# Three slots of modulated rows, and the second half's splits and stacks moved into attention, in the first block of an adaLN transformer kernel

## The chip, the cores and the metric

The kernel runs on one core of one Trainium2 chip. The metric is the device time of one execution in microseconds, as a median over runs. The engines are TensorE (PE, with its weight loads PEld), VectorE (DVE), ScalarE (ACT), GpSimd (POOL) and SyncE (SP), which here only issues transfers and waits. Each engine works through its own program in order; they meet at semaphores. Transfers are issued on the queue of the engine that issues them (SP or GpSimd) and run on 16 DMA engines.

## The reference

A transformer layer with adaptive layer norm over x of 8 blocks x 512 rows x 256 columns: relative-bias attention with 16 heads of 16, then a mixture of 8 experts of which each token takes 2. Six modulation vectors of 256 come for each block from one small product:

```python
mod = (_silu(L0_c) @ L0_wmod).reshape(L0_c.shape[0], 6, 1, -1)
sa, ca, ga, sb, cb, gb = (mod[:, 0], mod[:, 1], mod[:, 2], mod[:, 3], mod[:, 4], mod[:, 5])
ga = (2 * (ga >= 0) - 1) * jnp.maximum(jnp.abs(ga), 0.25)   # gb likewise
h = _layernorm(x, axis=-1) * (1 + ca) + sa
x = x + ga * attention(h)          # softmax(q k / 4 + bias[rel]) v, then W_out
h = _layernorm(x, axis=-1) * (1 + cb) + sb
x = x + gb * experts(h)            # top 2 of 8, gelu, layer norm, residual
```

## The kernel before

The kernel is four blocks of engine programs, one after the other: `prepare`, `attention`, `route`, `experts`. No engine starts a block before all have ended the one before. The change touches `prepare` and the first batch of `attention`.

`prepare` normalises and modulates the 8 blocks of x. For block b VectorE takes the moments of four 128-row tiles (`moments(b)`, L344 and L347), GpSimd raises variance to the power -0.5 (`deviations(b)`, L260 and L262), VectorE makes the offsets (`offsets(b)`, L352), ScalarE normalises the tiles (`normal(b)`, L297), TensorE transposes them (`turn(b)`, L456), and VectorE and ScalarE each apply scale and shift to one half of the transposed rows (`modulate(b)`, L359 and L305). Block 0 goes to a buffer that stays (`ahead.h1`); blocks 1 to 7 go to one of two slots of `ht`, from where GpSimd's queue stores them to `h1t` (`store_h(b)`, L268). A slot is used again when its store has landed (`stores_of_slot`).

Beside this, block 0's projections are made for the first batch of attention: TensorE multiplies q and k in halves (`project(k)`, L473; names `q0 k0 q1 k1 v0 v1` for k = 0 to 5), ScalarE adds the bias (`project_out`, L138), VectorE splits each result into three bf16 parts (`split(k)`, four passes, L368 to L374), SP stores the parts to `splits` (`store_parts`, L121) and, when the parts of one q and one k half have landed, loads them back as stacks of 96 rows (`load_stack`, L130: 6 loads for `qs`, 6 for `ks`, 128 KB each). Heads 0 to 7 use half 0, heads 8 to 15 half 1. SP also loads the bias rows of the heads as `s_tile`, four heads to a group (`load`, L151); groups 0 and 1 are loaded in `prepare`, 2 and 3 at the start of `attention`.

The modulation vectors are made twice. The columns for scale and shift come from sixteen small matmuls into `ps_col` (L489). The rows, which attention reads back from DRAM as `mod_rows`, come from three products of 512 columns (`mod(j)`, L481) into the one bank `ps_mod`, after `turn(3)`, `turn(4)` and `turn(5)` (`MOD_AFTER`); ScalarE copies each to `rows` (`copy_rows`, L317) after `modulate(2)`, (3) and (4), and VectorE makes the gates from them at the end (L433 to L443). SP then stores all six (L240) and waits until they have landed (`rows_stored`); that is SP's end of the block. GpSimd's end is the landing of all h1t stores. GpSimd also moves v into place and reloads h1 of block 1 (L272, L288), after `store_h(3)`.

In `attention` a batch is one block with 16 heads, n = 0 to 15. For each head TensorE makes four score tiles (L1183), VectorE adds the bias and takes the row minimum (L997), GpSimd and ScalarE subtract it, two tiles each (`lower`, L835 and L926), TensorE transposes (`turn_scores`, L1197, for head n - 1 in the time of head n), ScalarE takes exp (L934), TensorE weighs (L1211). GpSimd has further work at fixed places beside the heads (`beside(b, n, kind)`): it makes the splits of q and k for the next batch (`split_high`, `split_low`, L747 to L757) at n = 2 to 3.5 and 9.5 to 11, and at n = 5 it begins to split a piece of the expert weights (`piece_high(b, 0)`, L766, which waits for `w_piece_in[0]`). SP loads these pieces (`load_pieces`, L659). The order in SP's program for the first batch:

```python
if kind == "first":
    sp.wait_ge(h1_in, 16)
    for group in range(2, GROUPS):
        ahead.load(sp, ext_rows, group)
load_pieces(b, 0)
```

In GpSimd's program the work beside a head comes ahead of that head's subtractions: `beside(b, n, kind)`, `lower(b, n, 0)`, `lower(b, n, 1)`, `beside(b, n + 0.5, kind)`.

Of the kernel before, what the change touches and what calls it, by code (L numbers as in the profile page):

```python
# [158 lines left out]
def prepare(nc, ahead, x, c_t, wmod, rel_rev, w_qkv, b_qkv, w_out, b_out, gate_t, expert_bias, mod_rows, ext_rows, splits, h1t):  # L159

    with ExitStack() as ctx:  # L161
# [22 lines left out]
        ht = sb("ht", [P, 2, DC, S])  # L184
# [16 lines left out]
        h_out = [sem("h_out0"), sem("h_out1")]  # L201
        MOD_AFTER = (3, 4, 5)
        block = ctx.enter_context(nc.Block())

        def h1_of(b):

            return ahead.h1 if b == 0 else ht[:, b % 2, :, :]

        def stores_of_slot(b):

            return (b - 1) // 2 * 16 if b > 0 else 0

        @block.sync
        def _(sp):
# [8 lines left out]
            for b in range(1, B):  # L223
                load_x(b)

# [4 lines left out]
            ahead.load_weights(sp, w_qkv, b_qkv, w_out, b_out, gate_t, expert_bias)  # L230
# [13 lines left out]
        def _(pool):  # L244
# [19 lines left out]
            def store_h(b):  # L264

                pool.wait_ge(h_dve, b + 1)
                pool.wait_ge(h_act, b + 1)
                pool.dma_start(h1t[b, :, :, :], ht[:, b % 2, :, :]).then_inc(h_out[b % 2], 16)  # L268
# [8 lines left out]
            for b in range(1, B):  # L277
# [3 lines left out]
                if b == 3:  # L281
# [5 lines left out]
                    pool.wait_ge(h_out[1], 16)  # L287
                    pool.dma_start(ahead.h1[:, :, :], h1t[1, :, :, :]).then_inc(ahead.h1_in, 16)  # L288
            pool.wait_ge(h_out[0], 16 * (B // 2 - 1))
            pool.wait_ge(h_out[1], 16 * (B // 2))  # L290

        @block.scalar
        def _(act):
# [6 lines left out]
            def modulate(b):  # L300
# [3 lines left out]
                at_least(act, h_out[b % 2], stores_of_slot(b))  # L304
# [9 lines left out]
            def copy_rows(j):  # L314

                act.wait_ge(mod_ready, j + 1)
                act.activation(rows[:, j * 512:(j + 1) * 512], ps_mod[0:B, :], ACT.Copy).then_inc(rows_copied, 1)  # L317
# [3 lines left out]
            normal(0)  # L321
            normal(1)
            modulate(0)
# [15 lines left out]
        def _(dve):  # L339
# [15 lines left out]
            def modulate(b):  # L355

                dve.wait_ge(t_done, b + 1)
                at_least(dve, h_out[b % 2], stores_of_slot(b))
# [24 lines left out]

            dve.wait_ge(exp_done, 1)
# [17 lines left out]
            offsets(1)  # L402
            dve.wait_ge(cols_ready, 2)
            modulate(0)
            moments(2)
# [15 lines left out]
            split(2)  # L421
# [9 lines left out]
            dve.wait_ge(rows_copied, 3)  # L431
            for k, g in enumerate((2, 5)):
# [1597 lines left out]
```

## Time and profile before

| | us |
|---|---|
| median of 3 runs | 1262.36 |
| lowest, highest | 1259.53, 1264.88 |
| the profiled execution | 1260.16 |
| its span, first to last instruction | 1258.4 |
| first instruction of attention, from the span's start | 72.70 |
| TensorE's mean granted clock, as a share of 2.4 GHz | 0.942 |

The profile is of one execution; times inside it count from the span's start, and 1.8 us lie around the span. TensorE is busy for 1105.8 us (88%), VectorE for 790.0, GpSimd for 752.1, ScalarE for 632.7. A busy share over the whole span mixes the four blocks, so the stretches are read one by one. In the rows below an engine's idle time stands in brackets with what ended it; "DMA share" is the mean busy share of the 16 DMA engines, which can pass 1 when transfers overlap.

### The profile page before, as it was taken

The numbers are of one execution on the slowest core, as the hardware profiler recorded it, in microseconds if no ns is written. First come the engines' busy times: TensorE is split into PE (matmuls) and PEld (weight loads), VectorE is DVE, ScalarE is ACT, GpSimd is POOL, SyncE is SP. The second block draws the span as 40 slices with busy tenths as digits, with TensorE's granted clock in tenths as the row PEclk, the third lists the DMA queues.
The fourth block names the chain that finished last, engine by engine and source line by source line (L and its number), as shares of the span: only waits on it lengthen the run. The fifth ranks groups of instructions, "written<-read, shape, count | busy, mean of one in ns | idle before, by whom it ended". The sixth has DMA issues, their size and how long they took to land. (4 is left out here: it accounts for less than half of the span.)

```text
span 1258.4 us, 30706 instructions
## 1 busy us (share of the span) xinstructions
PE 1105.8 (88%) x11290; PEld 881.2 (70%) x11291; DVE 790.0 (63%) x2150; ACT 632.7 (50%) x905; POOL 752.1 (60%) x845
## 2 busy tenths in 40 slices
PE   5569999999999999999999826999999999999920
PEld 3237777777777777777777613888888888888820
DVE  4636668667676685776867676555555555555577
ACT  3538776776777777767677500222222222222222
POOL 2347497687776886759757521454554445554556
PEclk9779999999999999999999955999999999999965
DMA  8976754863557537555473156243434244242364
GB/s 281 297 217 181 209 154 109 198 143 100 142 144 173 146 92 187 144 112 171 90 185 102 68 170 183 42 113 49 117 44 111 46 117 115 44 112 46 50 172 138
DMA packets 124364, 167.18 MB, mean 133 GB/s; under 512 B 14520, under 2 KB 100792, under 8 KB 124256
## 3 DMA queue, kind: packets, MB, share of 16 engines
q1 hardware_dynamic: 107168, 137.59, 40.2%
q0 software_dynamic: 17088, 28.14, 12.1%
q8 instruction: 68, 1.11, 0.4%
q14 instruction: 40, 0.33, 0.1%
HBM read 105.26 MB, written 60.44 MB: 132 GB/s over the span
## 5 line engine op out<-in xcount | busy, mean ns | idle before, releaser
L997 DVE CUSTOM_DVE_ANT_0 b_sn<-b_ps_s,s_tile 128x512 f32<-128x512 f32 x512 | 341.3, 688 | 185.1 <-PE b_ps_s L1183 181.9
L934 ACT ACTIVATE b_pt<-b_ps_t 128x1024 f32<-128x1024 f32 x256 | 259.4, 1017 | 74.0 <-PE b_ps_t L1197 74.0
L1197 PE MATMUL b_ps_t<-ident,b_sn 128*128 128x128 f32 x2048 | 268.2, 273 | 3.1 <-POOL b_sn L835 1.3
L1197 PEld LDWEIGHTS b_ps_t<-ident,b_sn 128*128 128x128 f32 x2048 | 237.2, 141 | 41.0 <-issue 10.8
L1804 ACT ACTIVATE d_g<-d_ps_u 128x512 f32<-128x512 f32 x156 | 92.7, 598 | 308.2 <-PE d_ps_u L1930 300.2
L835 POOL TENSOR_SCALAR b_sn<-b_sn,b_mn 128x512 f32<-128x512 f32 x256 | 175.1, 695 | 97.2 <-DVE b_mn L997 96.7
L1759 POOL DMA_INDIRECT sums<-d_yo,d_places x78 | 132.4, 1698 | 166.2 <-ACT d_yo L1813 147.8
L926 ACT ACTIVATE b_sn<-b_sn,b_mn 128x512 f32<-128x512 f32 x256 | 181.9, 722 | 90.0 <-DVE b_mn L997 83.4
L1930 PE MATMUL d_ps_u<-d_xp,k_wu 128*128 128x256 bf16 x1776 | 202.0, 274 | 0.0
L1183 PE MATMUL b_ps_s<-s_ks,s_qs 96*128 96x512 bf16 x512 | 179.0, 386 | 24.8 <-PEq L161 14.7
L1945 PE MATMUL d_ps_y<-k_wd,d_gp 128*128 128x256 bf16 x1776 | 199.9, 273 | 0.0
L1930 PEld LDWEIGHTS d_ps_u<-d_xp,k_wu 128*128 128x128 bf16 x1776 | 173.5, 98 | 22.2 <-issue 0.4
L1945 PEld LDWEIGHTS d_ps_y<-k_wd,d_gp 128*128 128x128 bf16 x1776 | 173.8, 98 | 20.0
L1211 PE MATMUL b_ps_o<-b_pt,s_v 128*32 128x128 f32 x4096 | 138.4, 276 | 0.1
L1211 PEld LDWEIGHTS b_ps_o<-b_pt,s_v 128*32 128x32 f32 x4096 | 104.0, 109 | 40.8 <-ACT b_pt L934 36.8
L1842 DVE CAST d_xp<-d_ps_x 128x512 bf16<-128x512 f32 x39 | 26.9, 691 | 150.7 <-PE d_ps_x L1917 150.7
L1866 DVE TENSOR_TENSOR d_gp<-d_g,d_gp 128x512 bf16<-128x512 f32 x156 | 108.0, 692 | 5.4
L1739 POOL DMA_INDIRECT k_xg<-h_rows,d_tokens x76 | 76.0, 1000 | 43.5 <-POOL d_tokens L1735 31.8
L1864 DVE CAST d_gp<-d_g 128x512 bf16<-128x512 f32 x156 | 66.6, 427 | 39.3 <-ACT d_g L1804 35.9
L1183 PEld LDWEIGHTS b_ps_s<-s_ks,s_qs 96*128 96x128 bf16 x512 | 43.8, 98 | 57.2 <-DVE b_mn L997 36.2
L772 POOL TENSOR_TENSOR b_w_split<-b_w_raw,b_w_split 128x1024 bf16<-128x1024 f32 x32 | 68.8, 2148 | 0.0
L1228 PE MATMUL b_ps_m<-s_h,s_wqkv 128*128 128x512 f32 x112 | 54.4, 609 | 0.0
(239 smaller groups left out, 1126.2 us busy)
## 6 DMA issues: line engine op xcount, KB each, us to landing
w_parts<-b_w_split SPq DMA_DIRECT2D x32, 512.0 KB, 3.8
splits<-s_parts SPq DMA_DIRECT2D x32, 384.0 KB, 3.3
s_qs<-splits SPq DMA_DIRECT2D x96, 128.0 KB, 5.8
s_ks<-splits SPq DMA_DIRECT2D x96, 128.0 KB, 7.3
b_w_raw<-in_w_up_t SPq DMA_DIRECT2D x16, 512.0 KB, 10.8
b_w_raw<-in_w_down_t SPq DMA_DIRECT2D x16, 512.0 KB, 7.1
k_wu<-w_parts SPq DMA_DIRECT2D x8, 1024.0 KB, 4.9
k_wd<-w_parts SPq DMA_DIRECT2D x8, 1024.0 KB, 7.4
```

The source lines that it names most:

```text
L835: pool.tensor_scalar(sn[:, n % 2, t, :], sn[:, n % 2, t, :], -1.0, mn[:, n % 2, t:t + 1], ALU.mult, ALU.add).then_inc(lower_pool, 1)
L926: act.activation(sn[:, n % 2, t, :], sn[:, n % 2, t, :], ACT.Identity, bias=mn[:, n % 2, t:t + 1], scale=-1.0).then_inc(lower_act, 1)
L934: act.activation(pt[:, m, 2 * pair:2 * pair + 2, :], ps_t[:, 2 * pair:2 * pair + 2, :], ACT.Exp).then_inc(exped, 1)
L997: dve.tensor_tensor_reduce(sn[:, n % 2, t, :], ps_s[:, t % 2, :], ahead.tile[:, n, at:at + S], -1.0, BIG, ALU.add, ALU.min, mn[:, n % 2, t ...
L1183: pe.matmul(ps_s[:, t % 2, :], qs[:, half, m, t * P:(t + 1) * P], ks[:, half, m, :], start=True, stop=True).then_inc(scored, 1)
L1197: mm = pe.transpose(ps_t[:, j, t * P:(t + 1) * P], sn[:, m, t, j * P:(j + 1) * P], ident[:, :])
L1211: mm = pe.matmul(ps_o[2 * DK * t:2 * DK * (t + 1), n % TB * P:(n % TB + 1) * P], v[:, j, n, :], pt[:, n % 2, j, t * P:(t + 1) * P], start= ...
L1759: pool.indirect_dma_start(sums, bass.IndirectOffsetOnAxis(ap=places[:, u, i:i + 1], axis=0), yo[:, u, i, :], None, compute_op=ALU.add).the ...
L1804: act.activation(g[:, j, :], ps_u[:, j, :], ACT.Gelu).then_inc(gelued, 1)
L1866: dve.tensor_tensor(gp[:, u, 1, at], g[:, j, :], gp[:, u, 0, at], ALU.subtract).then_inc(g_split, 1)
L1930: mm = pe.matmul(ps_u[:, j // 2, j % 2 * ROWS:(j % 2 + 1) * ROWS], kept.wu[:, slot, w, c, j * P:(j + 1) * P], xp[:, u, x, c * ROWS:(c + 1) ...
L1945: mm = pe.matmul(ps_y[:, i, 0:D], gp[:, u, x, j * ROWS + i * P:j * ROWS + (i + 1) * P], kept.wd[:, slot, w, j, :], start=(j == 0 and n == ...
```

## The change

- `ht` gets three slots instead of two; block b uses slot (b - 1) % 3.
- SP issues `load_weights` (five small loads: biases, gate, w_out) between the loads of x for blocks 3 and 4, instead of after tile group 0.
- ScalarE does `modulate(0)` ahead of `normal(1)`, VectorE `modulate(0)` ahead of `offsets(1)`.
- TensorE multiplies a zeroed slot of `ht`, six times 128x512 before the column products and once after `turn(0)`; VectorE zeroes the slot first of all.
- The rows of modulation are two products instead of three (columns 512 to 1535), into `ps_mod` and `ps_col`, both after `turn(3)`; ScalarE copies them after `normal(5)`; the gates are made before `modulate(7)`; SP stores four of the six vectors, columns 512 on.
- GpSimd moves v and reloads h1 after `store_h(5)` instead of `store_h(3)`. Its `deviations` keep their places.
- The splits k = 2 and 3 of block 0 leave VectorE; GpSimd makes them in the first batch of attention at n = 0.5 and 1.5. SP stores them and loads the stack of half 1 at the start of that batch, ahead of tile groups 2 and 3 and of the first expert weights.

```diff
-        ht = sb("ht", [P, 2, DC, S])
+        HT = 3
+        ht = sb("ht", [P, HT, DC, S])
...
             for b in range(1, B):
                 load_x(b)
+                if b == 3:
+                    ahead.load_weights(sp, w_qkv, b_qkv, w_out, b_out, gate_t, expert_bias)
...
-            ahead.load_weights(sp, w_qkv, b_qkv, w_out, b_out, gate_t, expert_bias)
...
-            for k in range(2, 4):
-                ahead.store_parts(sp, splits, 0, k, k + 1)
-            ahead.load_stack(sp, splits, 0, 1)
             sp.wait_ge(rows_done, 1)
-            sp.dma_start(mod_rows, rows[:, :]).then_inc(rows_stored, 16)
+            sp.dma_start(mod_rows[:, 2 * D:], rows[:, 2 * D:]).then_inc(rows_stored, 16)
...
-                if b == 3:
+                if b == 5:
                     pool.wait_ge(ones_set, 1)
                     pool.wait_ge(v_out, 2)
...
             normal(0)
+            modulate(0)
             normal(1)
-            modulate(0)
...
             for b in range(3, B):
                 normal(b)
+
+                if b - 2 == MOD_AFTER:
+                    for j in range(2):
+                        copy_rows(j)
                 modulate(b - 1)
-                if b in MOD_AFTER:
-                    copy_rows(MOD_AFTER.index(b))
...
             moments(1)
-            offsets(1)
             dve.wait_ge(cols_ready, 2)
             modulate(0)
+            offsets(1)
...
             moments(6)
-            split(2)
             modulate(4)
             offsets(6)
             moments(7)
-            split(3)
             modulate(5)
             offsets(7)
             modulate(6)
+            make_rows()
             modulate(7)
...
+            def warm(n):
+
+                for _ in range(n):
+                    pe.matmul(ps_mod[:, :], ht[:, 2, 0, 0:P], idle, start=True, stop=True)
+
+            pe.wait_ge(idle_set, 1)
+            warm(WARM_FIRST)
             pe.wait_ge(silu_done, 1)
...
             turn(0)
+            warm(WARM_NEXT)
...
             for b in range(3, B):
                 turn(b)
-                if b in MOD_AFTER:
-                    mod(MOD_AFTER.index(b))
+                if b == MOD_AFTER:
+                    for j in range(2):
+                        mod(j)
...
                 if kind == "first":
 
+                    for k in range(2, 4):
+                        ahead.store_parts(sp, splits, 0, k, k + 1)
+                    ahead.load_stack(sp, splits, 0, 1)
                     sp.wait_ge(h1_in, 16)
                     for group in range(2, GROUPS):
                         ahead.load(sp, ext_rows, group)
...
                 first, last = kind == "first", kind == "last"
+                if first and n in (0.5, 1.5):
+                    split_high(2 + int(n), 2 + int(n), 0)
+                    split_low(2 + int(n), 2 + int(n))
```

## Rows read from the trace of the kernel before

**Rows 1.** Busy us by stretch and engine, granted clock, DMA share, GB/s.

```profile
60.00:65.00 5.00, 0.00 (x0) 0.00 (x0) 3.25 (x10) 0.50 (x1) 0.53 (x1) 0.50 1.14 168
...
100.00:150.00 50.00, 50.00 (x609) 37.94 (x608) 32.54 (x97) 39.28 (x49) 34.40 (x40) 1.00 0.71 218
```

**Rows 2.** Waits of SP and ScalarE to 85 us: total, times, longest.

```profile
SPq L127 <- DMA splits<-s_parts: 14.2, 2, 10.2
...
SPq L161 <- DMA mod_rows<-a_rows: 6.7, 1, 6.7
...
ACT a_rows L317 <- PE a_ps_mod L481: 10.2, 3, 4.0
```

**Rows 3.** Timeline of SP's queue: start, us of issuing, line, transfer, count.

```profile
27.15 3.96 SPq L121 DMA_DIRECT2D splits<-s_parts  x2
...
35.14 3.54 SPq L130 DMA_DIRECT2D s_qs<-splits  x6
...
41.67 2.15 SPq L151 DMA_DIRECT2D s_tile<-ext_rows  x4
...
58.44 3.15 SPq L130 DMA_DIRECT2D s_qs<-splits  x6
...
72.70 4.08 SPq L151 DMA_DIRECT2D s_tile<-ext_rows  x8
```

**Rows 4.** Stretches of 2 us, columns as in group 1.

```profile
44.00:46.00 2.00, 0.00 (x0) 0.00 (x0) 1.97 (x10) 2.00 (x5) 0.47 (x1) 1.00 1.12 158
...
52.00:54.00 2.00, 0.31 (x3) 0.32 (x4) 0.00 (x0) 2.00 (x5) 0.00 (x0) 1.00 1.02 416
...
152.00:154.00 2.00, 2.00 (x9) 0.99 (x8) 1.31 (x4) 1.28 (x3) 0.00 (x0) 1.00 1.18 131
```

**Rows 5.** Timeline of the first 30 us: start, us, engine, line, idle before.

```profile
14.87 0.36 DVE L347 BATCH_NORM_AGGREGATE a_mv<-a_stats 128x2 f32<-128x6 f32 x4
...
16.91 2.07 ACT L297 ACTIVATE a_xt<-a_xt,a_less,a_rstd 128x256 f32<-128x256 f32 x4 [4.86 <-DVE a_less L352]
...
19.79 5.49 PE L473 MATMUL a_ps_q<-s_h,s_wqkv 128*128 128x512 f32 x8 [5.21 <-ACT s_h L305]
...
24.36 0.43 DVE L368 CAST s_parts<-s_qf 128x512 bf16<-128x512 f32 x1 [5.16 <-ACT s_qf L138]
...
25.99 3.60 PE L473 MATMUL a_ps_q<-s_h,s_wqkv 128*128 128x512 f32 x8
```

**Rows 6.** Timeline, the last modulation of VectorE.

```profile
59.72 0.81 DVE L359 TENSOR_SCALAR a_ht<-a_ps_t,a_scale,a_shift 128x512 f32<-128x512 f32 x1 [3.63 <-DMA h1t<-a_ht]
```

**Rows 7.** DMA issues 40:50, 72:90: KB, us to landing; landings of h1t.

```profile
s_tile<-ext_rows SPq DMA_DIRECT2D x4, 448.0 KB, 11.9
...
splits<-s_parts SPq DMA_DIRECT2D x1, 384.0 KB, 2.5
...
DMA to landing us min/median/max: 3.7/4.2/8.5
```

**Rows 8.** Timeline of the first batch of attention, GpSimd and TensorE.

```profile
74.67 1.37 POOL L835 TENSOR_SCALAR b_sn<-b_sn,b_mn 128x512 f32<-128x512 f32 x2 [1.87 <-DVE b_mn L997]
...
96.38 1.06 POOL L766 CAST b_w_split<-b_w_raw 128x1024 bf16<-128x1024 f32 x1
...
98.92 1.37 POOL L835 TENSOR_SCALAR b_sn<-b_sn,b_mn 128x512 f32<-128x512 f32 x2 [1.49 <-DVE b_mn L997]
...
101.80 1.04 PE L1197 MATMUL b_ps_t<-ident,b_sn 128*128 128x128 f32 x8
...
116.67 0.61 POOL L747 CAST s_parts<-s_qf 128x512 bf16<-128x512 f32 x1 [0.36 <-ACT s_qf L138]
...
119.39 1.17 POOL L757 TENSOR_TENSOR s_parts<-s_rest,s_parts 128x512 bf16<-128x512 f32 x1
```

**Rows 9.** GB/s in 40 slices of 60:72, then of 72:90 us.

```profile
GB/s 263 379 191 106 157 133 116 137 161 106 137 157 106 126 222 184 205 358 427 386 393 365 314 167 140 171 150 171 147 164 157 150 188 133 174 147 65 55 0 0
...
GB/s 0 0 0 56 135 271 175 159 287 374 422 350 271 342 335 414 422 414 366 327 406 440 414 398 382 422 401 427 427 428 419 410 355 55 0 0 0 0 239 341
```

More of the change, by code:

```diff
@@ L200, in prepare @@
         bq_scaled, projected, qk_out, v_out = sem("bq_scaled"), sem("projected"), sem("qk_out"), sem("v_out")
-        h_out = [sem("h_out0"), sem("h_out1")]
-        MOD_AFTER = (3, 4, 5)
+        h_out = [sem("h_out0"), sem("h_out1"), sem("h_out2")]
+        MOD_AFTER = 3
+        WARM_FIRST, WARM_NEXT = 6, 1
+        idle = ht[:, 2, 0, :]
+        idle_set = sem("idle_set")
         block = ctx.enter_context(nc.Block())
         def h1_of(b):
-            return ahead.h1 if b == 0 else ht[:, b % 2, :, :]
+            return ahead.h1 if b == 0 else ht[:, (b - 1) % HT, :, :]
         def stores_of_slot(b):
-            return (b - 1) // 2 * 16 if b > 0 else 0
+            return (b - 1) // HT * 16 if b > 0 else 0
         @block.sync
@@ L285, in _ @@
                         move_v(half)
-                    pool.wait_ge(h_out[1], 16)
+                    pool.wait_ge(h_out[0], 16)
                     pool.dma_start(ahead.h1[:, :, :], h1t[1, :, :, :]).then_inc(ahead.h1_in, 16)
-            pool.wait_ge(h_out[0], 16 * (B // 2 - 1))
-            pool.wait_ge(h_out[1], 16 * (B // 2))
+            for slot in range(HT):
+                pool.wait_ge(h_out[slot], 16 * len(range(slot + 1, B, HT)))
         @block.scalar
@@ L316, in copy_rows @@
                 act.wait_ge(mod_ready, j + 1)
-                act.activation(rows[:, j * 512:(j + 1) * 512], ps_mod[0:B, :], ACT.Copy).then_inc(rows_copied, 1)
+                act.activation(rows[:, (j + 1) * 512:(j + 2) * 512], (ps_mod, ps_col)[j][0:B, :], ACT.Copy).then_inc(rows_copied, 1)
             act.wait_ge(c_in, 16)
@@ L382, in values, with make_rows @@
                                   ahead.b_v[:, :].unsqueeze(1).to_broadcast([P, 2, D]), ALU.add).then_inc(v_out, 1)
+            def make_rows():
+                dve.wait_ge(rows_copied, 2)
+                for k, g in enumerate((2, 5)):
+                    dve.tensor_scalar(sgn[:, k, :], rows[:, g * D:(g + 1) * D], 0.0, 2.0, ALU.is_ge, ALU.mult).then_inc(rows_step, 1)
+                for g in (4,):
+                    dve.tensor_scalar(rows[:, g * D:(g + 1) * D], rows[:, g * D:(g + 1) * D], 1.0, None, ALU.add).then_inc(rows_step, 1)
+                dve.wait_ge(rows_step, 3)
+                dve.tensor_scalar(sgn[:, :, :], sgn[:, :, :], -1.0, None, ALU.add).then_inc(rows_step, 1)
+                dve.wait_ge(rows_step, 4)
+                for k, g in enumerate((2, 5)):
+                    dve.tensor_tensor(rows[:, g * D:(g + 1) * D], rows[:, g * D:(g + 1) * D], sgn[:, k, :], ALU.mult).then_inc(rows_step, 1)
+                dve.wait_ge(rows_step, 6)
+                for k, g in enumerate((2, 5)):
+                    last = dve.scalar_tensor_tensor(out=rows[:, g * D:(g + 1) * D], in0=rows[:, g * D:(g + 1) * D], scalar=0.25,
+                                                    in1=sgn[:, k, :], op0=ALU.max, op1=ALU.mult)
+                last.then_inc(rows_done, 1)
+            dve.memset(idle, 0.0).then_inc(idle_set, 1)
             dve.wait_ge(exp_done, 1)
```

27 lines of the change are left out of this document (7 added, 20 removed).

## The prediction, written before the change was run

> **What bounds the kernel now.** I read the busy time by stretches first [rows 1]: from 100 us on TensorE is busy for 50.00 of 50 us, so whatever moves the start of attention moves the end by as much, and whatever stops TensorE there is lost in full. From 60 to 65 us TensorE does nothing and its granted clock is 0.50, the 1.2 GHz level: the first block waits for something else. The waits of the queue engine say for what [rows 2]: SP waits 10.2 us for two stores of split rows (half 1), then 6.7 us for mod_rows to land, and then the second block begins. SP's own timeline gives the order [rows 3]: stack of half 0 at 35.14, four bias tiles at 41.67, stack of half 1 only at 58.44, second block at 72.70. The bytes [rows 4] say why this is slow: while a stack of 12 loads is under way the core moves 158 GB/s (44 to 46 us) or 131 (152 to 154 us), with the DMA engines busy; otherwise 416.
>
> **The first block, part by part.**
> Early order. ScalarE no longer puts normal(1) ahead of modulate(0). Block 0's rows are complete when VectorE's modulate(0) ends; it now follows moments(1) at 15.2 us [rows 5], so at 16.0 instead of 19.7, and TensorE's q and k products, at 19.79 before [rows 5], start at about 16.1. ScalarE's normal(1) keeps 16.91 to 18.98, its first q output comes at 19.0 instead of 23.6, VectorE's split(0) at 19.75 instead of 24.36 [rows 5]: 4.6 us. Split(1) then ends near 26.2 instead of 30.7.
> Load_weights goes ahead of the loads of blocks 4 to 7: five issues of some 0.5 us and 0.56 MB, 1.4 us at 416 GB/s [rows 4]. Those four loads, the store of ext and tile group 0 move back by that much; block 4's moments come at 27 us, 7 us after its rows land, so I take nothing. The second store of split rows waits for split(1) and goes out at 27.1 instead of 31.1 [rows 3], but now behind group 0's 1.8 MB; it lands near 32 (35.1 before). So the stack of half 0 starts 3 us earlier.
> Idle products. Six of 128x512: at 0.86 us an instruction and two instructions each they end by 11.9 us at the latest, at most 2.6 us after w_mod (9.2). The columns are then done by 14.5, under the cover of moments(1), which hold VectorE to 15.2. Their use is that q and k run at 2.4 GHz: the eight instructions took 5.49 us at 19.79, after 5.2 us without work, and 3.60 at 25.99 [rows 5]. Without it q and k would end near 21.5, costing 1.5 us.
> Modulation. Three products with 10.2 us of ScalarE's waits for them [rows 2] become two, in two banks, copied two blocks later: no wait left. VectorE loses two splits (2.2 us each) and one row step. Three slots take away the waits for stores in modulate(5) and (7). Carried forward block by block at the durations of before, modulate(7) runs at 47 to 48 us instead of 59.72 [rows 6], rows_done at 46.8, the last store on GpSimd's queue goes out at 48 and lands, at 3.7 to 8.5 us [rows 7], at 52 to 56. Copying v and reloading h1 move behind store_h(5); nobody waits for them before TensorE's first product for block 1.
> SP's end. Stack from 32 for 11.3 us (35.14 to 46.4 before) to 43.3; tile group 1, issued behind it, was done 9.3 us after the stack (11.9 us after its issue at 41.67 to 43.8, [rows 3, 7]), beside GpSimd's stores; so 52.6; mod_rows, 32 KB, right behind, 54. With 0.5 us from landing to the first instruction, attention starts at **55.5 instead of 72.70: 17.2 us gained**, between 14 (rows at 416 GB/s without any gap give 57 to 58) and 19.5.
>
> **What attention takes over.** The split, the stores and the stack of half 1 now stand in the first batch, and two queues are moved past. T is the start of attention.
> GpSimd: two splits at heads 0.5 and 1.5. One costs 3.9 us (116.67 to 120.56, [rows 8]). Behind them wait the subtractions of heads 1 to 4, which TensorE's transposes need. GpSimd's first two end at T+3.35 (74.67 and 1.37 us); split 2 to T+7.2; head 1 to 8.6; split 3 to **T+12.5**. With the splits of block 1 it catches up at head 4; what it misses TensorE there is under 0.5 us, as each pair of subtractions had some 1.5 us to spare (100.29 to 101.80 for head 5).
> The trace has the first pass of a split at 0.43 us on VectorE [rows 5] and 0.61 on GpSimd [rows 8]. The Trainium skill ("GPSIMD Engine Reference", section 4.1) advises against such passes on GpSimd and puts two-input ones at about twice VectorE's time; by that a split of 2.2 us would take 4.4 and the chain below be 1 us later, but the 3.9 us are measured.
> SP: ahead of tile groups 2 and 3 and of the first expert weights (72.70 and, 4.08 us of issuing later, 76.8 before, [rows 3]) there now stand two stores that wait for GpSimd, and twelve stack loads that wait for these. Store to landing 2.5 us [rows 7] to 4.0 (31.1 to 35.14): T+15 to 16.5. Stack 1.57 MB: 11.3 us as in the first block, 12.3 at 131 GB/s [rows 4]: T+26.3 to 28.8. Eight tiles, 3.67 MB at 400 GB/s, 9.2 us: T+35.5 to 38. First weight piece 0.52 MB, 1.3 us: **T+36.8 to 39.3**. Stack and tiles are needed from head 8 on, three heads behind the stall below, so they are in time.
> The weight piece is not. GpSimd reads it at head 5 at T+23.7 (96.38, [rows 8]) and in order: the wait stands ahead of head 5's subtractions, which began at T+26.2. They now begin 1.06 us after landing, T+37.9 to 40.4, and TensorE's transposes for head 5 (101.80, T+29.1) 1 us after that: 9.8 to 12.3 us late. No other work of TensorE can pass. After 11 us without work its clock will be down, as from 60 to 65 us; what that costs is the difference of the two runs of q and k products, 5.49 less 3.60, 1.9 us [rows 5]. **Stall 11.5 to 14, middle 13.**
> The order within SP's queue carries this: in both stack stretches [rows 4] large loads stood issued behind the stack and the core still moved only 131 to 158 GB/s. The Trainium skill ("DMA: Bandwidth & Descriptors", section "Queues, rings and completion order") says the same, descriptors being consumed in ring order on each DMA engine; the trace agrees, and were they not, the result would be the first rival's.
>
> **Sum.** 17.2 gained, 13 lost: 4.2 us less. The profiled execution took 1260.2 us (span 1258.4 and 1.8 around it), giving 1256; the median of the runs, 1262.4, stands 2.2 above it, giving **1258**.
>
> **Rivals.**
> First, the weights are in time: tiles and weights pass beside the stack, landing by T+29, and the stall is under 4 us: 17.2 less 0 to 4, 1245 to 1249. For it: from 65 to 67 us a store of h1 rows brought the core to 358 to 427 GB/s beside a stack [rows 9]. Against: that was GpSimd's queue; SP's own did not [rows 4].
> Second, the gain is smaller: the block's end is set by bytes (seven stores of h1 rows, eight tiles, one stack, 10.2 MB from 24.5 us on) and by gaps while VectorE and ScalarE wait for slots; attention starts at 60. Gain 12.7, stall 13: 1262, no change. For it: DMA engines busy nearly throughout; against: 35.14 to 58.44 held about the same bytes.
> Third, slower: the queue ahead of the first weight piece takes longer, the stack at 110 GB/s (14.3 us) and the tiles at 350, the mean of 74 to 87 us (10.5, [rows 9]). It lands at T+42.8, TensorE stalls 17.5 us. With a gain of 17.2 this is break-even; that landing, T+42.5, is the point from which it decides. With a gain of 12 it is 5.5 more: 1268.
> That the change does not do what it says: GpSimd's roots hold the places they had in its program, only the copies of v and the reload moved; the sum rests on none of it.
>
> **Chances.** Forecast 0.60, its own range 1253 to 1262, of it 0.14 below 1256. First rival 0.15, second 0.11, third 0.14, of it 0.09 beyond the bound. A measurement of this kernel can tell about 0.5%, 6.3 us, from no change. Faster 0.14 + 0.15 = 0.29; slower 0.09; within 0.62. Range 1247 to 1266: it leaves out half of the first rival and some 0.06 of the third.
>
> **What would show it.** First instruction of attention at 53 to 58 us instead of 72.70; SP's wait for mod_rows before it short; VectorE's first split at 19.75; no wait of ScalarE for the products. In attention a single wait of GpSimd at head 5, on the load of w_up, of 12 to 15 us, TensorE idle beside it for 10 to 12 and a granted clock of 0.5 after it. The prediction is wrong if that wait is missing or if attention starts after 60.

## The result and the profile after

| | before | after |
|---|---|---|
| median, us | 1260.42 (20 runs) | 1265.52 (20 runs) |
| ratio, 95% interval | | 1.0039 [1.0031, 1.0047] |
| span of the profiled execution | 1258.4 | 1264.4 |
| first instruction of attention | 72.70 | 62.72 |
| weighing of block 0's last head on TensorE (L1211; L1235 after) | 155.94 | 161.71 |

The change made the kernel slower, by 5.1 us of the medians. That is less than the 6.3 us which the prediction took as its bound, but with 20 runs of each the interval does not reach a ratio of 1, so the kernel is slower. 1265.5 lies at the upper end of the stated range, and the forecast was 4.2 us in the other direction. The last two rows of the table split it: attention starts 9.98 us earlier, and the weighing of the sixteenth head of block 0 comes 5.77 us later. So 10.0 us were gained ahead of attention and 15.75 lost inside it.

SP's queue after (start, us of issuing, line, transfer, count), which answers to [rows 3]:

```profile
25.38 2.66 SPq L151 DMA_DIRECT2D s_tile<-ext_rows  x4
28.08 1.13 SPq L121 DMA_DIRECT2D splits<-s_parts  x2
40.78 3.27 SPq L130 DMA_DIRECT2D s_qs<-splits  x6
...
47.14 3.76 SPq L151 DMA_DIRECT2D s_tile<-ext_rows  x4
50.94 0.38 SPq L242 DMA_DIRECT2D mod_rows<-a_rows  x1
69.82 5.54 SPq L121 DMA_DIRECT2D splits<-s_parts  x2
77.58 2.69 SPq L130 DMA_DIRECT2D s_qs<-splits  x6
...
84.26 3.75 SPq L151 DMA_DIRECT2D s_tile<-ext_rows  x8
88.05 0.91 SPq L677 DMA_DIRECT2D b_w_raw<-in_w_up_t  x2
```

Two gaps stand out: 28.08 to 40.78, in which SP waits for the stores of split rows, and 50.94 to 62.72, in which it waits for mod_rows. The stack of half 0 starts 5.6 us later than before, though the second of its stores was issued 1.9 us earlier (29.2 against 31.1). From 69.82 on the order is the one forecast: stores, stack, eight tiles, weights.

The waits after (total us, times, longest), of SP, GpSimd and TensorE, for [rows 2]:

```profile
SPq L127 <- DMA splits<-s_parts: 13.6, 2, 11.5
SPq L161 <- DMA mod_rows<-a_rows: 11.0, 1, 11.0
...
POOL b_w_split L787 <- DMA b_w_raw<-in_w_up_t: 15.7, 1, 15.7
...
PE b_ps_t L1221 <- POOL b_sn L856: 13.3, 1, 13.3
```

The last two are the stall: GpSimd waits for the first piece of w_up, and TensorE for the subtraction behind it. ScalarE's 10.2 us for the modulation products are gone.

Stretches after, columns as in [rows 1]:

```profile
24.00:26.00 2.00, 1.70 (x11) 1.41 (x12) 1.90 (x4) 1.45 (x4) 1.45 (x1) 1.00 0.10 34
...
34.00:36.00 2.00, 0.54 (x5) 0.30 (x3) 1.47 (x8) 2.00 (x5) 0.91 (x3) 1.00 1.04 409
...
52.00:54.00 2.00, 0.00 (x0) 0.00 (x0) 0.00 (x0) 0.00 (x0) 0.00 (x0) 0.50 1.06 369
...
94.00:104.00 10.00, 0.00 (x0) 0.00 (x0) 0.00 (x0) 0.00 (x0) 1.20 (x2) 0.50 1.02 396
...
106.00:108.00 2.00, 2.00 (x10) 1.74 (x9) 0.57 (x1) 1.02 (x1) 2.00 (x2) 0.50 0.00 0
...
110.00:112.00 2.00, 2.00 (x31) 1.46 (x24) 0.59 (x3) 1.64 (x2) 1.72 (x1) 0.77 0.00 0
```

From 94 to 104 us TensorE, VectorE and ScalarE do nothing, at a granted clock of 0.50 (1.2 GHz), while 396 GB/s come in: the tiles and weights. TensorE then works, and the clock is still 0.50 in the stretches up to 110. At 52 to 54 no engine works either, while SP waits for mod_rows. At 24 to 26 the DMA engines are nearly idle (0.10): tile group 0 waits for the store of ext.

Single instructions after (start, us, engine, line, idle before), for [rows 5, 6, 8]:

```profile
15.87 3.67 PE L480 MATMUL a_ps_q<-s_h,s_wqkv 128*128 128x512 f32 x8 [0.18 <-DVE s_h L363]
...
19.44 0.43 DVE L372 CAST s_parts<-s_qf 128x512 bf16<-128x512 f32 x1 [1.13 <-ACT s_qf L138]
...
45.10 0.79 DVE L363 TENSOR_SCALAR a_ht<-a_ps_t,a_scale,a_shift 128x512 f32<-128x512 f32 x1
...
89.58 1.08 PE L1235 MATMUL b_ps_o<-b_pt,s_v 128*32 128x128 f32 x32
...
102.81 1.04 POOL L787 CAST b_w_split<-b_w_raw 128x1024 bf16<-128x1024 f32 x1 [15.68 <-DMA b_w_raw<-in_w_up_t]
...
104.66 2.12 PE L1221 MATMUL b_ps_t<-ident,b_sn 128*128 128x128 f32 x8 [13.28 <-POOL b_sn L856]
...
109.27 1.86 PE L1235 MATMUL b_ps_o<-b_pt,s_v 128*32 128x128 f32 x32
```

The early order worked: q and k at 15.87 instead of 19.79, the first split at 19.44 instead of 24.36, the last modulation at 45.10 instead of 59.72. Yet of the 14.6 us at the last modulation only 10 reach the block's end. Two weighings of the kernel before, the fourth and the fifth, price the stall below:

```profile
100.35 1.08 PE L1211 MATMUL b_ps_o<-b_pt,s_v 128*32 128x128 f32 x32
...
104.30 1.08 PE L1211 MATMUL b_ps_o<-b_pt,s_v 128*32 128x128 f32 x32
```

### The profile page after: what moved, and what is told of

Its sections match the earlier page's. It is cut to its first block and busy times, and to the rows that moved or that the text cites. A ratio compares the mean times of both kernels' runs of the same rounds, so it can differ in the third digit from the quotient of the medians.

```text
span 1264.4 us, 30726 instructions
## 1 busy us (share of the span) xinstructions
PE 1109.1 (88%) x11300; PEld 883.5 (70%) x11301; DVE 786.1 (62%) x2142; ACT 633.4 (50%) x904; POOL 759.9 (60%) x853
## 3 DMA queue, kind: packets, MB, share of 16 engines
q0 software_dynamic: 17088, 28.14, 12.2%
## 5 line engine op out<-in xcount | busy, mean ns | idle before, releaser
L1221 PE MATMUL b_ps_t<-ident,b_sn 128*128 128x128 f32 x2048 | 269.7, 274 | 16.5 <-POOL b_sn L856 15.3
L1207 PE MATMUL b_ps_s<-s_ks,s_qs 96*128 96x512 bf16 x512 | 179.8, 387 | 28.9 <-PEq L161 18.4
L1954 PEld LDWEIGHTS d_ps_u<-d_xp,k_wu 128*128 128x128 bf16 x1776 | 173.2, 98 | 21.9 <-issue 0.4
L1235 PE MATMUL b_ps_o<-b_pt,s_v 128*32 128x128 f32 x4096 | 139.1, 277 | 0.1
L1235 PEld LDWEIGHTS b_ps_o<-b_pt,s_v 128*32 128x32 f32 x4096 | 104.6, 110 | 41.2 <-ACT b_pt L958 36.8
```

The costliest lines, as they stand in the source:

```text
L1207: pe.matmul(ps_s[:, t % 2, :], qs[:, half, m, t * P:(t + 1) * P], ks[:, half, m, :], start=True, stop=True).then_inc(scored, 1)
L1221: mm = pe.transpose(ps_t[:, j, t * P:(t + 1) * P], sn[:, m, t, j * P:(j + 1) * P], ident[:, :])
L1235: mm = pe.matmul(ps_o[2 * DK * t:2 * DK * (t + 1), n % TB * P:(n % TB + 1) * P], v[:, j, n, :], pt[:, n % 2, j, t * P:(t + 1) * P], start= ...
L1954: mm = pe.matmul(ps_u[:, j // 2, j % 2 * ROWS:(j % 2 + 1) * ROWS], kept.wu[:, slot, w, c, j * P:(j + 1) * P], xp[:, u, x, c * ROWS:(c + 1) ...
```

## The experiments

Theory at the start: (a) the stall is set by what stands ahead of the first weight piece in SP's queue; (b) the block's end came late because the stores of split rows landed late, behind tile group 0 and beside GpSimd's stores of h1 rows. Rivals: for (a), that GpSimd with two more splits is the bound; for (b), that the block's end is bound by its bytes. All start from the changed kernel unless stated. In the table "attention" is the time of its first instruction, a ratio is to the runs of the kernel before that were taken beside it, and "(one)" marks a kernel that was run once. The stack and attention columns come from one profiled execution each. Four kernels have the same first block (changed, weights_first, pieces_first, stall_warm), and in them attention starts at 61.41 to 62.72: a difference of about 1.3 us between two kernels can be chance.

| kernel | stack of half 0 issued | attention | median, us | ratio to before |
|---|---|---|---|---|
| before | 35.14 | 72.70 | 1260.42 | 1 |
| changed | 40.78 | 62.72 | 1265.52 | 1.0039 [1.0031, 1.0047] |
| weights_first | 40.50 | 61.41 | 1252.94 | 0.9936 [0.9919, 0.9953] |
| pieces_first | 40.49 | 61.73 | 1248.77 | 0.9905 [0.9875, 0.9935] |
| pieces_parts_first | 29.86 | 59.31 | 1246.34 | 0.9881 [0.9852, 0.9910] |
| pieces_parts_hole | 29.12 | 59.18 | 1246.58 | 0.9882 [0.9852, 0.9911] |
| best_no_idle | 30.37 | 59.45 | 1246.83 | 0.9889 [0.9873, 0.9905] |
| parts_first | 29.98 | 58.85 | 1261.68 | 1.0013 [1.0003, 1.0023] |
| stores_late | 35.26 | 62.75 | 1265.69 (one) | |
| half1_back | 40.10 | 79.66 | 1265.88 | 1.0043 [1.0029, 1.0057] |
| half1_lw_back | 37.13 | 78.62 | 1265.05 (one) | |
| stores_beside | 37.44 | 76.46 | 1264.24 (one) | |
| before_half1_pieces | 34.98 | 63.59 | 1251.72 | 0.9929 [0.9912, 0.9945] |
| stall_warm | 40.29 | 62.05 | 1263.11 | 1.0020 [1.0010, 1.0030] |

**The stall: weights_first and pieces_first.**

```diff
-                    for k in range(2, 4):
-                        ahead.store_parts(sp, splits, 0, k, k + 1)
-                    ahead.load_stack(sp, splits, 0, 1)
                     sp.wait_ge(h1_in, 16)
...
                 load_pieces(b, 0)
+                if kind == "first":
+                    for k in range(2, 4):
+                        ahead.store_parts(sp, splits, 0, k, k + 1)
+                    ahead.load_stack(sp, splits, 0, 1)
```

> SP's program for the first batch: bias tiles of groups 2 and 3 and the first expert weights first, then the stores and the stack of half 1. Theory (GpSimd stands at head 5 because the weights are queued behind the stack): GpSimd's wait on w_up, 15.7 us in the changed kernel, and TensorE's wait of 13.3 us are gone, the start of attention stays at 62.7, the stack lands near T+28, before head 8 at T+36.8; the time falls by 13 to 16 us against the changed kernel, to 1250 to 1253. Rival (GpSimd is overloaded by its two additional splits, and the wait only shows it): TensorE still loses 5 us or more in heads 1 to 5, 1256 to 1260. Second rival (the stack comes late for head 8): TensorE waits there instead, and no more than half of the 16 us comes back.

The wait for w_up was gone, and 13 us with it (0.9936 against 1.0039). What was left, by the waits of GpSimd and TensorE in weights_first:

```profile
POOL s_parts L769 <- issue: 4.4, 1, 4.4
...
PE b_ps_t L1222 <- POOL b_sn L857: 2.9, 2, 2.8
```

The stores of half 1's split rows now stood behind 4.7 MB of tiles and weights, and GpSimd's next split waits for the slot that they empty; that this is the 4.4 us is read from the program, since the view names no releaser. So only the weights should pass (pieces_first moves `load_pieces` ahead of the stores, and leaves the tiles behind the stack):

> First batch of attention: only the two loads of expert weights ahead of the stores and the stack of half 1; tile groups 2 and 3 behind the stack as in the changed kernel. Theory (the stall is the place of the weights in SP's queue, and the 4.4 us wait of GpSimd for a parts slot in the run with tiles and weights first came from 3.7 MB of tiles ahead of the stores): neither wait is left, TensorE waits for nothing over 1 us in heads 1 to 8, the start of attention stays at 61.5 to 62.7, so 10 to 11 us below the kernel before: 1249 to 1251. Rival (two more splits on GpSimd cost TensorE time by themselves): 1252 to 1255, as with tiles and weights first.

```profile
61.73 0.81 SPq L677 DMA_DIRECT2D b_w_raw<-in_w_up_t  x2
68.82 5.54 SPq L121 DMA_DIRECT2D splits<-s_parts  x2
76.57 2.70 SPq L130 DMA_DIRECT2D s_qs<-splits  x6
...
83.33 3.77 SPq L151 DMA_DIRECT2D s_tile<-ext_rows  x8
```

This is SP's queue in pieces_first. The pieces land 3.9 us after issue, neither wait is left, and no wait of TensorE in the batch is longer than 0.7 us. From the start of attention to the weighing of the sixteenth head it takes 82.95 us (83.24 in the kernel before), so GpSimd's two extra splits cost nothing that shows. Theory (a) holds: 0.9905, from the order of one queue.

**The block's end: parts_first and stores_late.** parts_first puts the stores of split rows ahead of tile group 0:

```diff
-            ahead.load(sp, ext_rows, 0)
-
             for k in range(2):
                 ahead.store_parts(sp, splits, 0, k, k + 1)
+            ahead.load(sp, ext_rows, 0)
```

> In the first block SP issues the two stores of split rows ahead of bias tile group 0, all else as in the changed kernel. Theory (the stores landed at 40.8 us because 1.8 MB of tiles stood ahead of them in SP's queue): the stack of half 0 is issued from 30 to 32 us, attention starts at 54 to 57 instead of 62.7, and the stall stays, so 1257 to 1260. Rival (the stores lose to the stores of h1 rows on GpSimd's queue, which now fall into the same time): the stack is issued at 36 to 39, attention starts at 59 to 61, 1262 to 1264.

SP's queue in parts_first, its wait for mod_rows, and one stretch (columns as in [rows 1]):

```profile
25.50 1.17 SPq L121 DMA_DIRECT2D splits<-s_parts  x2
...
29.98 4.04 SPq L130 DMA_DIRECT2D s_qs<-splits  x6
...
45.84 0.34 SPq L241 DMA_DIRECT2D mod_rows<-a_rows  x1
```

```profile
SPq L161 <- DMA mod_rows<-a_rows: 12.3, 1, 12.3
```

```profile
52.00:54.00 2.00, 0.00 (x0) 0.00 (x0) 0.00 (x0) 0.00 (x0) 0.00 (x0) 0.50 1.03 421
```

The stack went out 10.8 us earlier, the end of the block only 3.9: mod_rows, issued at 45.84, waits 12.3 us behind bytes that pass at 342 to 421 GB/s from 46 to 58 us. From 26 us to the landing of mod_rows the core moves 10.3 MB in parts_first, in 32.5 us, and the same 10.3 MB in the changed kernel, in 36.3: the order of the stores moves the slow stretches, not the bytes. That the bytes are the bound is argued from these rates; no run takes them away. The rival of (b) takes over as soon as the split rows are early. In attention the stall is as long as before (TensorE waits 14.4 us), so the kernel gains 3.3 us by the ratios and no more.

stores_late holds GpSimd's stores of h1 rows until the split rows have landed:

```diff
-            for b in range(4):
+            for b in range(7):
                 deviations(b)
+            for k in range(2):
+                pool.wait_ge(ahead.parts_out[k], 16)
             for b in range(1, B):
                 store_h(b)
...
```

> GpSimd stores no h1 rows until both stores of split rows have landed; its roots for blocks 0 to 6 come ahead of that wait; all else as in the changed kernel. If the stores of h1 rows were what kept the split rows from landing: with 1.8 MB of tiles still ahead of them they land at 33 to 35 us and the stack is issued then. If it was the tiles alone: still at 39 to 41. The time itself tells little, as the stores of h1 rows then come later.

```profile
35.26 2.72 SPq L130 DMA_DIRECT2D s_qs<-splits  x6
```

The stack went out at 35.26 instead of 40.78 (40.1 to 40.8 in the five kernels that share this part): of the lateness some 5 us, 5.5 against the changed kernel, are those stores, which the early order had brought forward into the same stretch. Each on its own queue, they take bandwidth from each other. The Trainium skill ("DMA: Bandwidth & Descriptors", "Queues, rings and completion order") says that a DMA engine takes turns between the queues that have work for it; the 5.5 us agree. Held back, the stores cost as much at the end (62.75).

**Half 1 left in the first block: half1_back, half1_lw_back, stores_beside.** half1_back undoes the move of half 1 and keeps the rest of the change:

```diff
             ahead.load(sp, ext_rows, 1)
+            for k in range(2, 4):
+                ahead.store_parts(sp, splits, 0, k, k + 1)
+            ahead.load_stack(sp, splits, 0, 1)
...
+            split(2)
             modulate(4)
...
+            split(3)
             modulate(5)
...
-                    for k in range(2, 4):
-                        ahead.store_parts(sp, splits, 0, k, k + 1)
-                    ahead.load_stack(sp, splits, 0, 1)
...
-                if first and n in (0.5, 1.5):
-                    split_high(2 + int(n), 2 + int(n), 0)
-                    split_low(2 + int(n), 2 + int(n))
```

> The splits, stores and stack of half 1 are back in the first block (splits on VectorE), the rest of the change stays: three slots, early order, idle products, two modulation products. Theory: no stall in attention, but the first block ends with the stack of half 1 again, at 70 to 74 us, so what the rest is worth is 0 to 3 us: 1258 to 1263. If the rest were worth its 4.6 us of earlier splits at the end of the block, attention starts at 68 and the time is 1255 to 1257.

Not what was expected: attention at 79.66, 7.0 us later than before the change. That execution took 1268.37 us, 2.5 above the median of its five runs; by the ratio the kernel is 5.4 us slower. By themselves, the third slot, the early order and the rest make the block longer. Moving half 1 then brings 16.9 us (79.66 to 62.72) and costs about as much in the stall. half1_lw_back also puts `load_weights` back behind tile group 0:

> Half 1 back in the first block, and the loads of biases, gate and w_out back behind tile group 0; three slots, early order, idle products and two modulation products stay. With half 1 back alone the stack of half 0 was issued at 40.1 us and attention started at 79.7 (72.7 before). If the loads of biases and weights, put ahead of the loads of x, did that: tile group 0 at 22.7, stack at 34 to 36, attention at 72 to 74. If the stores of h1 rows did it, which now come 5 us earlier and compete with the split rows: stack at 38 to 40, attention at 77 to 79.

The stack of half 0 went out at 37.13 instead of 40.10, between the two expectations, but attention starts only 1.0 us earlier, which is within chance: the place of the small loads is worth 3 us at the stack and little at the block's end. stores_beside holds the stores of h1 rows 6 and 7, in half1_lw_back, until the split rows of half 1 have landed:

```diff
             for b in range(1, B):
+                if b == 6:
+                    for k in range(2):
+                        pool.wait_ge(ahead.parts_out[k], 32)
                 store_h(b)
```

> The kernel half1_lw_back (half 1 and load_weights back in their old places in the first block, the rest of the change kept; attention at 78.62 us, in the kernel before at 72.70), and GpSimd holds its stores of h1 rows 6 and 7 until both stores of split rows of half 1 have landed. Theory: the rest of the change made the block longer because these two stores, which the third slot brings forward, run ahead of the split rows and not beside the slow stack of half 1, where the kernel before has them; held back they run beside the stack again, the stack of half 1 is issued at 57 to 61 us (64.07 without the hold) and attention starts at 72 to 76. Rival: the order on SP's queue and the late splits cause it, not GpSimd's stores: the stack is issued at 63 to 66 and attention starts at 78 or later.

A stretch under the stack of half 1, first of half1_lw_back, then of stores_beside (columns as in [rows 1]; the last one is GB/s):

```profile
70.00:72.00 2.00, 0.00 (x0) 0.00 (x0) 0.00 (x0) 0.00 (x0) 0.00 (x0) 0.50 1.18 127
```

```profile
66.00:68.00 2.00, 0.00 (x0) 0.00 (x0) 0.00 (x0) 0.00 (x0) 0.00 (x0) 0.50 1.04 347
```

Between the two expectations: attention at 76.46, 2.2 us earlier, of the 5.9 that half1_lw_back has over the kernel before. The third slot lets these stores run ahead of the split rows and leaves the stack by itself, at 127 GB/s. Beside it they pass nearly free, as before the change [rows 9]: from the issue of the stack to attention it takes 14.40 us with the two stores (62.06 to 76.46) and 14.55 without (64.07 to 78.62). That accounts for 2.2 us, from one execution of each. Of the other 3.8, 2.3 stand already at the stack of half 0 (37.44 against 35.14), where stores_late would suggest the stores of h1 rows again, though it was not tried in this kernel; 1.5 stay open.

**What the rest is worth without half 1: before_half1_pieces.** The kernel before, with half 1's splits, stores and stack moved as in the change and the weights ahead as in pieces_first, and no other edit.

> The kernel before with only half 1 moved to attention (its two splits on GpSimd at heads 0.5 and 1.5, its stores and stack in the first batch), and the first expert weights ahead of them as in pieces_first; nothing else of the change. It tells what the other edits of the first block are worth once half 1 has left it; with them (pieces_first) attention started at 61.73 us and the ratio was 0.9905. Theory: the early order and the third slot still bring the end forward there, since VectorE's modulate(7) waited for a store's landing until 59.72 in the kernel before: attention at 63 to 67 us, ratio 0.992 to 0.996. Rival: as in half1_back they cost 5 us or more by sending the stores of h1 rows ahead of the split rows; then attention starts at 55 to 60 us and the ratio is 0.985 to 0.989.

As the theory had it: attention at 63.59, ratio 0.9929. The block's end waits there for VectorE (wait of SP; then VectorE's timeline):

```profile
SPq L237 <- DVE a_rows L438: 17.7, 1, 17.7
```

```profile
49.76 0.81 DVE L356 TENSOR_SCALAR a_ht<-a_ps_t,a_scale,a_shift 128x512 f32<-128x512 f32 x1 [4.31 <-DMA h1t<-a_ht]
```

So the waits of two slots still cost. The other edits (pieces_first, 61.73) take them away, bring GpSimd's last store of h1 rows from 58.73 to 46.54, and gain 1.9 us at attention, little more than chance, where with half 1 in the block they lose 7.0.

**The best of both: pieces_parts_first, pieces_parts_hole, best_no_idle.** pieces_parts_first joins the edits of pieces_first and parts_first:

> The same, and the stores of split rows ahead of tile group 0 in the first block. If the end of the first block is what remains: attention starts at 58.9 as with the stores first alone, and 3 to 4 us fall off once more: 1245 to 1248. If a byte bound shows elsewhere (the stack of half 1 late for head 8): no gain over the weights first.

GpSimd's first piece of weights and the subtractions behind it, no wait ahead of the piece:

```profile
83.61 1.04 POOL L788 CAST b_w_split<-b_w_raw 128x1024 bf16<-128x1024 f32 x1
84.83 1.36 POOL L857 TENSOR_SCALAR b_sn<-b_sn,b_mn 128x512 f32<-128x512 f32 x2 [0.18 <-DVE b_mn L1022]
```

Span 1244.5, 13.9 us below before, and attention starts 13.4 earlier: nothing of the gain is given back. Its runs, 1245.76 to 1246.53 us, all lie below those of pieces_first (1248.09 to 1250.29), and no kernel of the study has a lower median. pieces_parts_hole also moves the five small loads behind the store of ext, so that they fill the idle DMA engines there:

> The same, and the loads of biases, gate and w_out not between the loads of x but behind the store of ext, in the 3 us in which SP waits for that store and the DMA engines move 34 GB/s. If the block's end is bound by bytes with that gap in them: tile group 0 and attention come 1.5 to 3 us earlier, 56 to 57.5, 1243 to 1246. If it is bound by the chain of VectorE and ScalarE or by the stack: no change.

```profile
22.69 3.85 SPq L121 DMA_DIRECT2D splits<-s_parts  x2
26.58 2.07 SPq L151 DMA_DIRECT2D s_tile<-ext_rows  x4
```

Nothing: the stack went out at 29.12 instead of 29.86, attention at 59.18. But the hole was not filled, only moved. Tile group 0 stands behind the second store of split rows, which waits for VectorE's split(1), done at 26.14; so the group went out at 26.58, against 26.36 in pieces_parts_first, and the core moves 131, 155 and 169 GB/s in the three stretches from 24 to 30 us (34, 290 and 242 there). The run does not tell bytes from the chain of engines. best_no_idle takes the seven idle products out (`WARM_FIRST, WARM_NEXT = 0, 0`):

> The kernel pieces_parts_first (1246.34 us, ratio 0.9881, attention at 59.31 us) without TensorE's seven idle products in the first block. Theory: without them TensorE makes q0 and k0 at the low clock, 5.5 us instead of 3.67, so split(0) and split(1) of VectorE begin 1.5 to 2 us later and with them the stores of split rows; the stack of half 0 is issued 1 to 2 us later and attention starts 0.5 to 2 us later: ratio 0.9885 to 0.9905. Rival: the block's end is set by the bytes between, and the idle products are worth nothing: attention within 0.5 us of 59.3, ratio 0.987 to 0.989.

```profile
16.16 5.74 PE L479 MATMUL a_ps_q<-s_h,s_wqkv 128*128 128x512 f32 x8 [1.62 <-DVE s_h L362]
```

TensorE's timeline in best_no_idle: q and k take 5.74 us, against 3.67 in pieces_parts_first. VectorE's second split ends 1.16 us later (27.08 against 25.92), the stack goes out 0.5 later, attention starts 0.14 later. The rival holds: the 2 us at q and k are real, and worth nothing that shows at the block's end. (The granted clock of this trace reads 1.00 there, so the durations alone show them.) Nor do the idle products bring them each time: in pieces_first, parts_first and pieces_parts_hole, which have them, q and k took 4.62 to 4.67 us at a granted clock of 0.50 up to 18 us.

**The price of the low clock: stall_warm.** The stall stays; TensorE is kept busy in it.

```diff
+                    if kind == "first" and n == 6:
+                        pe.wait_ge(freed, 2)
+                        for _ in range(14):
+                            pe.matmul(ps_m[:, :], ident[:, :], wqkv[:, 0, 0:S], start=True, stop=True)
                     if kind != "first" or n > 0:
                         turn_scores(h - 1, (n + 1) % 2, 0)
```

> The changed kernel, with 14 products of 128x512 that nobody reads put on TensorE ahead of the transposes of head 5 in the first batch; the wait itself stays. At about 0.87 us each they fill 12.2 of the 13.3 us in which TensorE stood idle. Theory: the stall costs what TensorE starts late (12.8 us) and some 3 us more because it works on at a granted clock of 0.50 until 110 us; with the clock kept up, the transposes still begin at 104 to 106 us, at a granted clock near 1.00, the ones of head 5 take 1.04 us and not 2.12, and the x load that stands at 158.61 us comes 2 to 3 us earlier; the time is 2 to 3 us below the changed kernel's, a ratio to before of 1.0015 to 1.0025. Rival: after the stall GpSimd and VectorE set the pace with their own backlog and TensorE's clock costs nothing; then the load stays within 0.7 us of 158.6 and the ratio at 1.0035 to 1.0045.

TensorE's timeline in stall_warm, and one stretch (columns as in [rows 1]):

```profile
90.36 12.18 PE L1326 MATMUL b_ps_m<-s_wqkv,ident 128*128 128x512 f32 x28
104.60 0.41 PE L1221 MATMUL b_ps_t<-ident,b_sn 128*128 128x128 f32 x2 [2.06 <-POOL b_sn L856]
...
107.30 1.08 PE L1235 MATMUL b_ps_o<-b_pt,s_v 128*32 128x128 f32 x32
```

```profile
106.00:108.00 2.00, 2.00 (x38) 1.60 (x40) 1.11 (x3) 1.75 (x2) 2.00 (x2) 1.00 0.00 0
```

TensorE worked through the wait, and the granted clock was 1.00 after it (0.50 in the changed kernel). Between the fourth weighing and the fifth it lost 14.62 us (88.73 to 107.30, against 3.95 in the kernel before), of it 14.4 by late transposes, and 0.26 more up to the sixth; at the sixteenth head it stands 13.91 us behind the kernel before, counted from the start of attention, and not 15.75. The ratio fell by 0.0019, which is 2.4 us. So the theory's price holds; the two intervals, 1.0010 to 1.0030 and 1.0031 to 1.0047, just fail to meet. The x load on SP's queue that was to come 2 to 3 us earlier came only 1.3 earlier, at 157.31: the weights landed 0.6 us later in this execution, and SP's load is no clean marker; the weighings are.

## Why the prediction was wrong, step by step

**What bounds the kernel: right.** TensorE is busy throughout attention, and both terms, the earlier start and the stall, went into the span in full: 9.98 gained, 15.75 lost, 5.77 later at the sixteenth head, 6.0 in the span.

**Early order: right in the engines.** Split at 19.44 (19.75 forecast), q and k at 2.4 GHz (3.67 us), last store of h1 rows issued at 46.19 (48), no wait for the products, no long one for slots. That these gains reach the block's end was the mistake.

**Landing of the split rows near 32: the step that failed.** They landed at 40.7, 11.5 us after the last issue. The sum put only tile group 0's 1.8 MB ahead of them. It left out the stores of h1 rows that the early order itself brings forward. GpSimd's queue in the changed kernel, then in the kernel before:

```profile
26.96 0.80 POOL L270 DMA_DIRECT2D h1t<-a_ht  x1 [1.46 <-DVE a_ht L363]
...
30.88 0.64 POOL L270 DMA_DIRECT2D h1t<-a_ht  x1 [1.12 <-DVE a_ht L363]
...
33.95 0.61 POOL L270 DMA_DIRECT2D h1t<-a_ht  x1 [0.28 <-issue]
...
38.14 0.62 POOL L270 DMA_DIRECT2D h1t<-a_ht  x1 [1.23 <-ACT a_ht L307]
```

```profile
31.89 0.80 POOL L268 DMA_DIRECT2D h1t<-a_ht  x1 [1.46 <-DVE a_ht L359]
...
35.78 0.64 POOL L268 DMA_DIRECT2D h1t<-a_ht  x1 [1.11 <-DVE a_ht L359]
...
40.50 0.61 POOL L268 DMA_DIRECT2D h1t<-a_ht  x1 [1.91 <-ACT a_ht L305]
```

From 26 to 40.8 us the core moved 4.7 MB: 2.6 on SP's queue (1.8 of tiles, 0.8 of split rows) and 2.1, four stores of h1 rows, on GpSimd's. From 38 to 40.8 us SP's queue moved 0.04 MB of that and GpSimd's 0.86: the last packets of the split rows landed among the stores. stores_late puts 5.5 of the 8.8 us on these stores. 2.7 more is tile group 0 itself, issued at 25.38 instead of 22.68, since the store of ext waits behind the small loads and the loads of x (DMA share 0.10 at 24 to 26 us); the text moved it back by 1.4. In half1_lw_back, with the small loads in their old place, the group went out at 22.83 and the stack 3.0 us earlier than in half1_back.

**The 17.2 us of gain were wrong for a second reason.** Of the 7.2 us between 55.5 and 62.72 the landing carries about half. parts_first and the three kernels built on it put the stack at 29.12 to 30.37, earlier than the text had it, and attention still starts at 58.85 to 59.45: 3.3 to 3.9 us earlier than in the changed kernel, and 3.3 to 4.0 later than forecast. The text took 23.5 us from the issue of the stack to attention, out of durations of the kernel before. The changed kernel has 21.9 there, which looks well sized, but the four with the early stack have 28.9 to 30.1. As far as the rates show it, the reason is in the bytes: between the issue of the stack and the landing of mod_rows the changed kernel moves 5.6 MB, parts_first 9.3, since most of tile group 0, and 4.2 MB of GpSimd's queue instead of 2.1, now pass after the issue of the stack. From 46 to 58 us no engine has more than 0.81 us of work in a stretch of two, and the queues move 342 to 421 GB/s. That is the second rival's mechanism. For these kernels the lower end of the text's own range (14 us of gain, 58.7), taken from rows at 416 GB/s, was the right value, and the chance of 0.11 for that rival was too low: the block has as many bytes as before less one stack and its stores, and an earlier engine moves none of them away.

**The stall: right in its place, mechanism and order, too small by some 3 us.** GpSimd's wait at head 5 on w_up: 15.7 us. Split 3 ended at T+12.3 (12.5), the stack went out at T+14.9 (15 to 16.5), and ran to about T+28 (26.3 to 28.8). Then two things were mis-sized. The first piece landed at T+39.9 (36.8 to 39.3): the two pieces of w_up land 14.6 and 15.4 us after their issues, so they come in side by side, and 4.72 MB at the 385 GB/s of that stretch are 12.3 us where the sum had one piece and 10.5. The transposes came 13.6 us late after the fourth weighing (12.8 by the start of attention, as the first heads ran 0.8 us ahead of those before); the text had 9.8 to 12.3. And the low clock cost 2.9 us: 2.1 between the transposes and the fifth weighing (4.61 us, 2.50 before) and 0.8 up to the sixth (4.96 against 4.17); the text had 1.9. stall_warm leaves 0.5 of the 2.9. In all 13.6 + 2.9 = 16.5, less the 0.8, is 15.75, against a middle of 13. Three sums of the text are off without weight in the result: 1.57 MB at 131 GB/s are 12.0 us, not 12.3; the small loads hold 0.54 MB, not 0.56; and with the two-input passes alone doubled a split of 2.2 us becomes 3.6, not 4.4 (3.9 measured). The 2.2 us that it added to reach a median of three runs are gone in the 20.

**The rivals.** The first, weights in time, did not come: tiles and pieces did not pass beside the stack. With tiles issued from 84.26 on, the core still moved 133 GB/s from 86 to 88 us. The third had the right sign. It named a landing at T+42.5 as decisive, with the gain held at 17.2; the landing was T+39.9, short of it, and the kernel is slower all the same, since the gain was 10.0 and the break-even moved with it. It also named a joint case, a gain of 12 with a stall of 17.5, 5.5 us slower, close to the 5.8 measured at the sixteenth head. That is luck: it rested on a stack at 110 GB/s and tiles at 350, which moved 133 to 138 and 396, and on no cause for the smaller gain. What was not priced is that both terms miss together, each inside its own doubt: a gain at 60 us (12.7) with the upper stall (14) gives 1.3 us slower. In both terms the queues carried more bytes than were counted, 2.1 MB of stores in the one and a second piece of 0.5 MB in the other.

**The change as a whole.** half1_back and before_half1_pieces show that its parts don't add up. With half 1 in the first block the other edits cost 7.0 us of the block's end; without it they gain 1.9, and 2.4 more with the split rows ahead of tile group 0 (61.73 to 59.31). Moving half 1 is what pays, if the weights pass it in SP's queue. Open: 3.8 us of the 7.0, of which 2.3 arise ahead of the stack of half 0; how much of the block's end with the early stack is bytes and how much the chain of engines; and why the first heads of attention ran 0.8 us ahead.

## What to carry to other kernels

When work moves from one stage into the next, read the order of each queue that it is put into, and price what stands behind it there: moving a 1 MB load ahead of a stack and eight tiles turned 0.4% slower into 1% faster. A stage that is waiting for bytes is shortened little by making its engines earlier: 12.2 us at the last store of h1 rows were 1.9 at the block's end (before_half1_pieces, pieces_first). Count the bytes of all queues between two landings, and ask which stores an earlier engine will send into that stretch. Price the rivals together as well as one at a time, since one cause can move both terms of a sum.

## What the runs showed of the hardware

- After 13.3 us without work TensorE resumed at 104.66; its granted clock was 0.50 in the stretches up to 110 us, 0.77 from 110 to 112 and 1.00 from 112 to 114. With products in the wait (stall_warm) it was 1.00 from 104 us on, and the kernel was 2.4 us faster.
- A stack by itself moved 127 GB/s at a DMA share of 1.18 (half1_lw_back), and with two stores of h1 rows beside it, from the other queue, the core moved 347 GB/s at 1.04 (stores_beside). Here a slow transfer left room for another queue's, though not for its own: with tiles issued behind the stack on the same queue the core stayed at 133 (changed kernel).
- Split rows of 0.79 MB landed 11.5 us after issue behind 1.8 MB of tiles and beside four stores of 0.5 MB (changed kernel), 7.4 us after it behind the tiles alone (stores_late), and 3.3 us after it when they were first (parts_first).
